# A fused vision kernel on one core: its attention and gating slots reordered, mixing and memsets moved

## The reference, cut to what matters

```python
h = _L0_tok_ref(x, ...)                                   # patches -> tokens of 192, (64 images, 49 tokens)
h = h + _L0_attn_ref(_layernorm(h), ...)                  # windows attention at several scales, Gelu, @ ow.T
h = h + _L0_ffn_ref(_layernorm(h), ...)                   # the part that the change is in:

xn = _layernorm(x, norm1_w, norm1_b)
q, k, v = split(xn @ qkv_w.T + qkv_b)                     # 12 heads of 16
attn = softmax(einsum('bhqd,bhkd->bhqk', q, k) * scale)   # 49 x 49 for each head
x = x + (einsum('bhqk,bhkd->bqhd', attn, v) @ proj_w.T + proj_b)
xn2 = _layernorm(x, norm2_w, norm2_b)
top_vals, top_idx = top_k(xn2 @ w_gate, 2)                # 8 experts, the best two for each token
gates = softmax(top_vals)
moe = sum over experts e of gate_e * (gelu(xn2 @ W1[e] + b1[e]) @ W2[e] + b2[e])
return x + moe
```

## Time and profile before

| | us |
|---|---|
| median of 3 runs | 1188.52 (1186.59 to 1189.37) |
| the profiled execution | 1187.29, its span 1185.5 |
| PE busy | 999.9 (84%) |
| DVE busy | 678.8 (57%) |
| ACT busy | 452.6 (38%) |
| POOL busy | 545.3 (46%) |

### The profile page before, as it was taken

The page is one execution under the profiler, slowest core; times in us unless marked ns, Lnnn a source line. Parts: engine busy times, 40 slices in busy tenths (PEclk is TensorE's granted clock), DMA queues, the critical chain, the costliest instruction groups (busy, mean ns, idle before and its releaser), DMA issues.

```text
span 1185.5 us, 23992 instructions
## 1 busy us (share of the span) xinstructions
PE 999.9 (84%) x6992; PEld 860.4 (73%) x6993; DVE 678.8 (57%) x1791; ACT 452.6 (38%) x1140; POOL 545.3 (46%) x1047
## 2 busy tenths in 40 slices
PE   6969999999997987489888888888629999999960
PEld 4768899889875654377767777677518999999960
DVE  5465576585436788646788878888532222222216
ACT  1233233324113444323555555555204434343424
POOL 1385677586521222213566666666512333343430
PEclk9989999999988998789999999999659999999995
DMA  8447562561102400302600000000011111111118
GB/s 347 165 173 303 219 243 93 215 268 64 37 11 53 68 1 0 56 1 86 268 16 15 15 15 15 15 15 19 21 50 34 43 41 44 37 42 41 44 33 252
DMA packets 41701, 103.09 MB, mean 87 GB/s; under 512 B 7046, under 2 KB 28656, under 8 KB 38837
## 3 DMA queue, kind: packets, MB, share of 16 engines
q1 hardware_dynamic: 30085, 88.86, 21.6%
q0 software_dynamic: 5760, 9.68, 2.4%
q10 hardware_dynamic: 5808, 3.96, 1.1%
HBM read 86.30 MB, written 18.32 MB: 88 GB/s over the span
## 4 chain that ended last, share of the span: by engine, by line
PE 44%; issue 17%; POOLq 13%; DVE 10%; POOL 7%; DMA 4%; DVEq 2%; ACT 2%; SPq 1%; ACTq 0%
PE pe L1602 15%; PE pp L967 5%; PE pe L951 4%; PE pe L1611 3%; POOLq L559 3%; POOLq L537 2%; PE pe L954 2%; POOLq L526 2%; DMA x<-yy_d 2%; POOL xs_d L529 1%; POOL xn L532 1%; POOL hall L540 1%; POOLq L510 1%; DVE sc L316 1%; PE pe L183 1%
## 5 line engine op out<-in xcount | busy, mean ns | idle before, releaser
L1602 PE MATMUL pe<-wm,xm 128*128 128x193 f32 x1008 | 174.2, 332 | 1.2 <-DVEq L1406 1.2
L1602 PEld LDWEIGHTS pe<-wm,xm 128*128 128x128 f32 x1008 | 168.4, 193 | 5.6 <-issue 4.0
L834 ACT ACTIVATE hT<-pe,eb 128x128 f32<-128x128 f32 x336 | 92.7, 375 | 147.5 <-PE pe L954 147.5
L967 PE MATMUL pp<-w2s,hT 128*128 x672 | 118.5, 327 | 0.0
L967 PEld LDWEIGHTS pp<-w2s,hT 128*128 128x128 f32 x672 | 107.9, 191 | 0.2
L951 PE MATMUL pe<-xsT,ew 128*128 128x128 f32 x672 | 90.1, 286 | 3.5 <-ACT xsT L824 3.5
L756 DVE TENSOR_TENSOR ys<-pp,b2s 128x192 f32<-128x192 f32 x56 | 20.0, 358 | 124.8 <-PE pp L967 124.8
L951 PEld LDWEIGHTS pe<-xsT,ew 128*128 128x128 f32 x672 | 81.7, 197 | 8.7 <-ACT xsT L824 4.1
L555 POOL DMA_INDIRECT yy_d<-ys,yix x56 | 65.4, 1168 | 46.4 <-issue 46.4
L529 POOL DMA_INDIRECT xs_d<-xsrc,dst x64 | 65.4, 1022 | 41.6 <-issue 41.6
L1331 POOL TENSOR_TENSOR sqs<-sqs,sqt 128x448 f32<-128x448 f32 x56 | 67.9, 1212 | 8.0
(11 more groups left out here) (273 smaller groups left out, 2316.1 us busy)
## 6 DMA issues: line engine op xcount, KB each, us to landing
xm<-in_xm SPq DMA_DIRECT2D x7, 2688.0 KB, 15.2
raw<-in_xwa SPq DMA_DIRECT2D x7, 1792.0 KB, 7.5
raw<-in_xwb SPq DMA_DIRECT2D x7, 1536.0 KB, 10.9
x<-in_x SPq DMA_DIRECT2D x4, 1536.0 KB, 8.9
xs<-xs_d SPq DMA_DIRECT2D x56, 96.5 KB
x<-yy_d SPq DMA_DIRECT2D x8, 672.0 KB
w1s<-in_W SPq DMA_DIRECT2D x1, 4608.0 KB
w2s<-in_W SPq DMA_DIRECT2D x1, 4608.0 KB
```

The costliest lines, as they stand in the source:

```text
L834: last = f(self.hT[:, u, c], pe1[:, 2 * u + c % 2, (c // 2) * ROWS:(c // 2 + 1) * ROWS], ACT.Gelu, bias=self.b1[:, u, c:c + 1])
L967: last = mm(pp[:, u, 0:D], self.hT[:, u, n], self.w2s[:, bass.ds(e, 1), n * D:(n + 1) * D].rearrange("p o d -> p (o d)"), start=(n == 0), ...
L1602: mm(y[:, 0:D + 1], cell(q, c), wm[:, q, c], start=(q + c == 0), stop=(q == 3 and c == KC - 1))
```

## The change

Four things are changed, all in the pair slots and just ahead of them.

1. `clear` moves from DVE to POOL, with a drain after each memset. POOL does it when DVE has finished with the windows (`qkv_free`), ahead of `pads`. DVE and PE wait for `init` only after mix pieces 0 and 1.
2. DVE's slot: the maxima of the scores first, with a drain behind them and the subtraction at once; bn_stats, `xn` and bn_aggr of the other stages come after. The results' product goes to bank 0.
3. The results' transposes and ACT's copy of them (n2, end of the slot) become n3's, at the beginning of the next slot, behind the scores on PE and ahead of exp on ACT. DVE waits for c_T before it writes `on`. On PE the projection comes ahead of the transposes of the probabilities. These are made in two parts (blocks 4 and 5 into bank 0, blocks 0 to 3 into bank 1), and copied and multiplied part by part.
4. The mix pieces of slots 0 to 4: two (2 and 3; 4 and 5; 7 and 8; 10 and 11; 13 and 14) stand behind QKV on PE and behind `x` on DVE, one (6, 9, 12, 15, none in slot 0) at the end of the slot.

```diff
 Windows.vector
-        self.clear(dve)
 Heads.gpsimd
-        pool.wait_ge(self.init, 2)
+        pool.wait_ge(self.wins.qkv_free, NWT)
+        self.clear(pool)
         pool.wait_ge(self.wins.so_out, NWT)
 Heads.clear
-        dve.drain()
-        v.memset(self.pm[:], 0.0)
-        v.memset(self.vbd[:], 0.0)
+        def put(t, value):
+            g.memset(t, value)
+            pool.drain()
+        pool.drain()
+        put(self.pm[:], 0.0)
+        put(self.vbd[:], 0.0)
...
-        dve.drain().then_inc(self.init, 2)
+        pool.drain().then_inc(self.init, 2)
 Heads.vector
         self.mixed(dve, range(2))
+        dve.wait_ge(self.init, 2)
...
             dve.drain()
-            if n6 is not None:
-                v.max(self.m8[:], lg[:])
-            if n0 is not None:
-                v.bn_stats(self.bn[:, 0], row(hall, n0))
             if n2 is not None:
                 dve.wait_ge(self.b_s, n2 + 1)
                 sc = pe1[:, 0:2, 0:6 * T].rearrange("p n (h k) -> p n h k", h=6)
                 v.tensor_reduce(self.mx2[:].rearrange("p (n h) -> p n h", n=2), sc, X, ALU.max)
+            if n6 is not None:
+                v.max(self.m8[:], lg[:])
+            dve.drain()
+            if n2 is not None:
+                v.tensor_tensor(self.pm[:]..., sc, self.mx2[:]..., ALU.subtract).then_inc(self.b_sub, 1)
+            if n0 is not None:
+                v.bn_stats(self.bn[:, 0], row(hall, n0))
...
-            if n2 is not None:
-                v.tensor_tensor(self.pm[:]..., sc, self.mx2[:]..., ALU.subtract).then_inc(self.b_sub, 1)
...
                 v.tensor_scalar(row(x2, n0), row(hall, n0), st[:, 0:1], st[:, 2:3], ALU.subtract, ALU.mult).then_inc(self.a_x, 1)
+                if isinstance(n0, int) and n0 < 5:
+                    self.mixed(dve, [3 * n0 + 1, 3 * n0 + 2] if n0 else [2, 3])
...
-            o = pe1[:, 1, 0:AH * (AHD + 1)].rearrange("p (h d) -> p h d", h=AH)
+            o = pe1[:, 0, 0:AH * (AHD + 1)].rearrange("p (h d) -> p h d", h=AH)
...
             if n2 is not None:
+                dve.wait_ge(self.c_T, n2)
                 v.tensor_tensor(self.on[:]..., o[:, :, 0:AHD], ..., ALU.mult).then_inc(self.b_on, 1)
...
-            if isinstance(n0, int) and n0 < 5:
-                self.mixed(dve, range(3 * n0 + 2, min(3 * n0 + 5, NP // 2)))
+            if isinstance(n0, int) and 0 < n0 < 5:
+                self.mixed(dve, [3 * n0 + 3])
 Heads.scalar
+            if n3 is not None:
+                act.wait_ge(self.c_T, n3 + 1)
+                act.wait_ge(self.c_proj, n3)
+                f(self.onT[0:H2], pe1[0:H2, 2, 0:2 * P]..., ACT.Copy).then_inc(self.c_out, 1)
             if n2 is not None:
                 act.wait_ge(self.b_sub, n2 + 1)
...
-                act.wait_ge(self.b_pT, n2 + 1)
-                f(self.pT[:, 0:4]..., pe1[:, 0], ACT.Copy)
-                f(self.pT[:, 4:6]..., pe1[:, 1, 0:2 * P], ACT.Copy).then_inc(self.b_pTo, 1)
+                for k, (lo, hi) in enumerate(((4, 6), (0, 4))):
+                    act.wait_ge(self.b_pT, 2 * n2 + k + 1)
+                    f(self.pT[:, lo:hi]..., pe1[:, k, 0:(hi - lo) * P], ACT.Copy).then_inc(self.b_pTo, 1)
...
-            if n2 is not None:
-                act.wait_ge(self.c_T, n2 + 1)
-                f(self.onT[0:H2], pe1[0:H2, 2, 0:2 * P]..., ACT.Copy).then_inc(self.c_out, 1)
 Heads.tensor
-        pe.wait_ge(self.init, 2)
...
         self.mix(pe, range(2))
+        pe.wait_ge(self.init, 2)
...
                 last.then_inc(self.b_s, 1)
+            if n3 is not None:
+                pe.wait_ge(self.b_on, n3 + 1)
+                pe.wait_ge(self.c_var, n3)
+                for h in range(2):
+                    last = T_(pe1[0:H2, 2, h * P:(h + 1) * P], self.on[:, h * H2:(h + 1) * H2], ident)
+                last.then_inc(self.c_T, 1)
...
                 last.then_inc(self.a_qkv, 1)
+            if isinstance(n0, int) and n0 < 5:
+                self.mix(pe, [3 * n0 + 1, 3 * n0 + 2] if n0 else [2, 3])
...
-            if n2 is not None:
-                pe.wait_ge(self.b_ex, n2 + 1)
-                for n in range(6):
-                    last = T_(pe1[:, n // 4, (n % 4) * P:(n % 4 + 1) * P], self.pm[:, 2 * n:2 * n + 2]..., ident)
-                last.then_inc(self.b_pT, 1)
             if n3 is not None:
                 pe.wait_ge(self.c_out, n3 + 1)
                 ...
+            if n2 is not None:
+                pe.wait_ge(self.b_ex, n2 + 1)
+                for part in ((4, 5), (0, 1, 2, 3)):
+                    for n in part:
+                        last = T_(pe1[:, 1 - n // 4, (n % 4) * P:(n % 4 + 1) * P], self.pm[:, 2 * n:2 * n + 2]..., ident)
+                    last.then_inc(self.b_pT, 1)
...
-                pe.wait_ge(self.b_pTo, n2 + 1)
                 pe.wait_ge(self.a_v, n2 + 1)
-                for m in range(2):
-                    for n in range(6):
-                        last = mm(pe1[m * B:(m + 1) * B, 1, n * w:(n + 1) * w], ...)
+                for k, part in enumerate(((4, 5), (0, 1, 2, 3))):
+                    pe.wait_ge(self.b_pTo, 2 * n2 + k + 1)
+                    for n in part:
+                        for m in range(2):
+                            last = mm(pe1[m * B:(m + 1) * B, 0, n * w:(n + 1) * w], ...)
...
-            if n2 is not None:
-                pe.wait_ge(self.b_on, n2 + 1)
-                pe.wait_ge(self.c_var, n2)
-                for h in range(2):
-                    last = T_(pe1[0:H2, 2, h * P:(h + 1) * P], self.on[:, h * H2:(h + 1) * H2], ident)
-                last.then_inc(self.c_T, 1)
-            if isinstance(n0, int) and n0 < 5:
-                self.mix(pe, range(3 * n0 + 2, min(3 * n0 + 5, NP // 2)))
+            if isinstance(n0, int) and 0 < n0 < 5:
+                self.mix(pe, [3 * n0 + 3])
```

More of the change, by code:

```diff
@@ L564, in gpsimd, with clear @@
         run_slots(pool, NT, 5, expert)
-    def clear(self, dve):
-        v = self.nc.vector
-        dve.drain()
-        v.memset(self.pm[:], 0.0)
-        v.memset(self.vbd[:], 0.0)
-        dve.drain()
-        v.memset(self.vbd[0:T, :, :, AHD:AHD + 1], 1.0)
-        v.memset(self.vbd[B:B + T, :, :, 2 * AHD + 1:2 * AHD + 2], 1.0)
-        v.memset(self.acc[:], 0.0)
-        for t in (self.xT2, self.onT, self.qT, self.xnT2):
-            v.memset(t[H2:P].rearrange("p a n -> p (a n)"), 0.0)
-        v.memset(self.kbd[H2:P].rearrange("p m h g t -> p (m h g t)"), 0.0)
-        v.memset(self.zero[:], 0.0)
-        dve.drain()
-        v.memset(self.xT2[H2:H2 + 1, 1], 1.0)
-        v.memset(self.onT[H2:H2 + 1, 1], 1.0)
-        dve.drain()
-        v.memset(self.zero[:, D:DX], float(FAR))
-        dve.drain().then_inc(self.init, 2)
+    def clear(self, pool):
+        g = self.nc.gpsimd
+        def put(t, value):
[4 more added lines that the diff above has]
+        put(self.vbd[:], 0.0)
+        put(self.vbd[0:T, :, :, AHD:AHD + 1], 1.0)
+        put(self.vbd[B:B + T, :, :, 2 * AHD + 1:2 * AHD + 2], 1.0)
+        put(self.acc[:], 0.0)
+        for t in (self.xT2, self.onT, self.qT, self.xnT2):
+            put(t[H2:P].rearrange("p a n -> p (a n)"), 0.0)
+        put(self.kbd[H2:P].rearrange("p m h g t -> p (m h g t)"), 0.0)
+        put(self.zero[:], 0.0)
+        put(self.xT2[H2:H2 + 1, 1], 1.0)
+        put(self.onT[H2:H2 + 1, 1], 1.0)
+        put(self.zero[:, D:DX], float(FAR))
+        pool.drain().then_inc(self.init, 2)
     def vector(self, dve):
@@ L775, in slot @@
         def slot(item):
-            n0, n1, n2, n5, n6 = (item(lag) and item(lag)[0] for lag in (0, 1, 2, 5, 6))
+            n0, n1, n2, n3, n5, n6 = (item(lag) and item(lag)[0] for lag in (0, 1, 2, 3, 5, 6))
+            if n3 is not None:
+                act.wait_ge(self.c_T, n3 + 1)
+                act.wait_ge(self.c_proj, n3)
+                f(self.onT[0:H2], pe1[0:H2, 2, 0:2 * P].rearrange("p (h n) -> p h n", h=2), ACT.Copy).then_inc(self.c_out, 1)
             if n2 is not None:
@@ L806, in slot @@
                 last.then_inc(self.a_v, 1)
-            if n2 is not None:
-                act.wait_ge(self.c_T, n2 + 1)
-                f(self.onT[0:H2], pe1[0:H2, 2, 0:2 * P].rearrange("p (h n) -> p h n", h=2), ACT.Copy).then_inc(self.c_out, 1)
             if n5 is not None:
@@ L894, in slot @@
                 last.then_inc(self.c_nT, 1)
-            if n2 is not None:
-                pe.wait_ge(self.b_ex, n2 + 1)
-                for n in range(6):
-                    last = T_(pe1[:, n // 4, (n % 4) * P:(n % 4 + 1) * P], self.pm[:, 2 * n:2 * n + 2].rearrange("p h k -> p (h k)"), ident)
-                last.then_inc(self.b_pT, 1)
             if n3 is not None:
@@ L909, in slot @@
             if n2 is not None:
-                pe.wait_ge(self.b_pTo, n2 + 1)
                 pe.wait_ge(self.a_v, n2 + 1)
                 w = 2 * (AHD + 1)
-                for m in range(2):
-                    for n in range(6):
```

(7 more changed lines are left out.)

10 lines of the change are left out of this document (5 added, 5 removed).

## The result

| | before | after |
|---|---|---|
| median of 5 runs | 1189.37 us (1186.59 to 1190.80) | 1176.57 us (1174.75 to 1180.30) |
| profiled execution, its span | 1187.29, 1185.5 | 1176.30, 1174.5 |

A forecast was written before the change was run, and what follows sets the result against it. The prediction took POOL's closed loop with DVE as the bound from about 575 to 823. Terms -1.8-7.8-1.3+1.2+0-3.8, stated as -13.7, took 1187.29 to 1173.6; the median being 1.2 higher, 1174.8 us, range 1164 to 1183.

The forecast's parts named there:

- Memsets: Start to the first mix: clearing on POOL instead of DVE lets L354 start at 478.2, gaining 1.8 us.
- The row that the sum went by: L354's sixteen adds stay at 10.9 us beside POOL's memsets; with contention up to 3.5 us would come back.
- Front: First mix to first scores: moved mix pieces cut 28.8 us to 21.0, -7.8, with half clock until about 505.
- Slots 2 to 4: Pair slots 2, 3 and 4 would take 10.75, 11.7 and 11.75 us: -1.25, -0.45 and +0.6.
- Slots 5 to 7: Slots 5 and 6 gain 0.1 and 0.15 us; slot 7 loses 1.2 once, L630 coming later.
- The steady slots: The 24 or so slots at POOL's pace: no change per slot; bounds 0.6 gained or 0.5 lost each.
- rival C: Steady slots: DVE late at c_r in every slot, 0.8 us each, 19 in all; 1194 us, chance 0.08.
- POOL's lap: Steady slots: the closed loop L507, L538, `xn`, L630, L507 sets the 9.94 us rhythm.
- D: Steady slots: other DVE operations delay POOL's scatter preparation, 0.3 us a slot, 7 in all; 1182 us, chance 0.09.
- The end: From 823: POOL's waits for c_var shrink, gaining 3.8 us; bounds 1.9 and 5.1.
- A: Steady slots: TensorE's waits for exp are the bound and go, 14 us more gained; 1160 us, chance 0.12.
- B: Front: clock low through slot 1, -4 instead of -7.8, and half the end's gain; 1180.5 us, chance 0.13.

The follow-up runs named there:

- e1: The kernel before with only the memsets on POOL and the mix pieces moved, old slot order kept; 1183.02 us, ratio 0.9908.
- e9: e3 plus nine filling products ahead of the first transposes and four ahead of the first QKV; 1168.64 us, ratio 0.9800.
- e11: e1 plus VectorE's new slot order only, PE and ACT in their old order; 1188.14 us, ratio 0.9991 against the kernel before.
- e3: The kernel after plus six unread matmuls on TensorE between the weighted sum and the wait for xh; 1168.25 us, ratio 0.9779.
- e6: e3 without POOL's multiplication by the norm's weights (L520); 1154.57 us, ratio 0.9689 against the kernel before.
- e4: The kernel before without POOL's multiplication by the norm's weights (L520); 1209.19 us, ratio 1.0112.
- e2: The kernel after with memsets and mix pieces as before, only the slot order new; 1189.83 us, ratio 0.9964 against the kernel before.
- e12: The kernel after with VectorE's old order at the head of the slot, PE's and ACT's new; 1176.98 us, ratio 0.9898 against the kernel before.

## Why the prediction was right, and which of its steps were not

*Memsets.* L353 starts at 477.48 (478.2 forecast). Less the 0.74 us that are not the change's, the first mix is 1.65 earlier; -1.8 was right. The row that the sum went by held as well: 10.96 for 10.93. The contention that the Trainium skill names (GPSIMD Engine Reference, 1. Specifications) isn't seen with these memsets. The weights were no limit: the first QKV waited for ACT's copy (L808), 0.94 us.

*Front.* -8.28 for -7.8, with the first QKV at half clock from 500.55 to 504.67 (3.18 + 1.31 us), where the forecast had 500.7 to 505. e1 shows that the front alone brings slot 7 forward by 9.5 of the 10.8 us, and e9 that the half clock costs 1.66.

*Slots 2 to 4* came at 10.00, 10.83 and 10.83 for 10.75, 11.7 and 11.75: the term was mis-sized. It took the busy time of the old order as the work. TensorE was busy for 9.74, 10.57 and 10.57 in them, 0.5 to 0.7 less than the terms took. The weighted sum's 24 products take 1.38 in the old order (e11) and 1.07 in the new one (after's L932 at 546.56), which is 0.3 in each slot; the rest was not followed. The idle time was 0.26 in each, not 0.45 to 0.5.

*Slots 5 to 7* came at +0.26, +1.05 and +2.19 for -0.1, -0.15 and +1.2. The difference in slots 6 and 7 is the clock: the scores at 549.58 and 559.59 take 2.23 and 2.24 us. The +1.2 of slot 7 is there, with 1.0 of slow scores on top. So slots 2 to 7 came to -0.14 for -0.15, by errors that cancel.

*The steady slots* are the step that failed: "So 0 for each slot: the exponential that comes 1.2 us sooner only moves idle time." It moved idle time, 25 us of it, but to a place where TensorE's clock fell, and the slot went from 9.96 to 10.15, +4.51. The prediction has the granted clock for the front alone, and takes it as full in the steady slots without a reason. The bound given for a loss, 0.5 a slot, holds it; its mechanism (DVE late at c_r, rival C) is not what happened, since DVE waits 1.4 us for c_r in all, in three slots. The sign that the prediction named as wrong, a rhythm outside 9.8 to 10.1 and no wait of DVE for L538, is what was seen. The claim that POOL's lap is the bound was half right: e3 and e6 show it for the new order with the clock held, while e4's slots at clock 1.00 suggest that in the old order another lap stood beside it, so that "PE's chain needs some 8.5" was too low there. That the time came out all the same is in part luck: of the 4.51 lost here, 1.48 came back where no term had them and 1.1 in the first two rows.

*Slot 7 to 8* gained 1.48 that no term had. Before, 11.69 us, with 2.36 us ahead of the slot's first scatter; after, 10.21 with 1.02. e1 took 10.24, e2 10.46, e12 12.16. It comes and goes with no part of the change, and its cause was not tried. (The prediction's rows for D begin at 584 and so leave this scatter out.)

*The end* was -3.22 for -3.8, and comes with the slot order (e1 +0.2, e2 -4.7). POOL no longer waits for c_var there, as forecast; late next was `xn`, for which POOL waits 2.28 us once (L520 at 826.78).

*The rivals.* A would have given 1160: its lap is shorter, but with the clock down nothing came of it, and with the clock held e3 stayed at POOL's 9.95. B: the clock was at half for the first QKV only; the mix pieces behind it, from 504.67, ran at full speed (0.49 us a row for 0.85), so B's condition did not arise. D: the idle time ahead of the scatters is 27.1 us in 46 of them, 0.59 each, what it was.
